# Graph layer, destination pass: record windows of 192 rows with two neighbouring rows on a partition

## What is computed

```python
# layer 0: attributes of the edges, summed at their source node
seg_sum, seg_max, cnt = segments of edge_attr (50000 x 32) by src
seg_mean = seg_sum / maximum(cnt, 1);  seg_max = where(cnt > 0, seg_max, 0)
x = x + relu(concat(seg_sum, seg_max, seg_mean, u) @ W1 + b1) @ W2 + b2
# layer 1: features of the source nodes, summed at the destination node
h = relu(layernorm(x))
x = x + relu(segment_sum(h[src], dst) @ W.T + b)
```

## Time and profile before

| | us |
|---|---|
| median of 3 runs | 1623.49 |
| lowest and highest run | 1609.49, 1625.28 |
| span of the profiled execution | 1619.7 |

### The profile page before, as it was taken

One profiled execution on the slowest core, in us unless ns is written; L12 is line 12 of the kernel. 1 busy time (PEld: TensorE's weight loads), 2 busy tenths in 40 slices (PEclk: granted clock), 3 DMA queues, 4 the chain that ended last, 5 costly groups with the idle time before them and its releaser, 6 DMA issues.

```text
span 1619.7 us, 28924 instructions
## 1 busy us (share of the span) xinstructions
PE 880.8 (54%) x8466; PEld 635.9 (39%) x8466; DVE 995.8 (61%) x2746; ACT 552.6 (34%) x1726; POOL 848.1 (52%) x863
## 2 busy tenths in 40 slices
PE   0120145787888788888795113545455445455553
PEld 0010022555555555565574102433334333333442
DVE  9899944677777777778795113444455444444553
ACT  0300123444444444444451213333344333333430
POOL 4733175566656666666610755555566555555400
PEclk9985556899989989889998555555555555555555
DMA  1000012688777877777797114787688767887889
GB/s 42 0 0 0 15 39 57 159 224 225 206 199 201 218 211 209 206 205 214 215 256 225 27 31 100 180 203 176 161 184 195 174 165 178 201 189 180 190 204 205
DMA packets 486483, 253.92 MB, mean 157 GB/s; under 512 B 417657, under 2 KB 449373, under 8 KB 486323
## 3 DMA queue, kind: packets, MB, share of 16 engines
q1 hardware_dynamic: 376066, 157.65, 39.3%
q10 hardware_dynamic: 85168, 75.08, 15.4%
q0 software_dynamic: 25088, 19.32, 7.0%
HBM read 159.45 MB, written 92.43 MB: 156 GB/s over the span
## 4 chain that ended last, share of the span: by engine, by line
ACT 20%; ACTq 19%; another core or an unknown queue 18%; issue 16%; DVE 15%; PE 9%; DMA 2%; SPq 1%; POOL 1%; DVEq 0%; POOLq 0%
ACTq L680 10%; ACT hn L759 6%; ACT xa L665 4%; ACTq L712 3%; ACTq L686 3%; ACT rec L706 3%; ACT hid L693 2%; ACTq L673 2%; DVE ka L976 2%; DVE kb L976 2%; ACT rec L700 2%; DVE ka L977 2%; DVE kb L977 1%; PE p_m L1428 1%
## 5 line engine op out<-in xcount | busy, mean ns | idle before, releaser
L589 POOL DMA_INDIRECT xa<-node_table,gi x392 | 370.7, 946 | 340.8 <-ACT hn L759 142.5
L577 POOL DMA_INDIRECT xa<-in_edge_attr_dram,gi x392 | 402.0, 1026 | 266.7 <-issue 94.9
L759 ACT ACTIVATE hn<-xa,nmr,rstd 128x64 f32<-128x64 f32 x392 | 140.4, 428 | 340.9 <-issue 292.0
L1228 DVE RECIPROCAL rstd<-sd 128x4 f32<-128x4 f32 x98 | 17.5, 178 | 303.9 <-ACT sd L751 210.5
L700 ACT CAST rec<-p_m 128x256 bf16<-128x256 f32 x164 | 60.7, 370 | 292.7 <-remote 259.6
L1480 PE MATMUL p_g<-ident,hn 128*128 128x128 f32 x196 | 64.9, 431 | 156.1 <-ACT hn L759 94.8
L1125 DVE TENSOR_TENSOR_SCAN feats<-c_rows,feats,p_g 64x512 f32<-64x512 f32 x97 | 122.9, 1267 | 16.4 <-PE p_g L1412 8.2
L693 ACT ACTIVATE hid<-p_z,bias_z 128x512 f32<-128x512 f32 x98 | 113.1, 1154 | 53.9 <-issue 23.2
L1428 PE MATMUL p_m<-w_s,hid 128*128 128x64 f32 x784 | 121.2, 300 | 6.6 <-issue 6.5
L1127 DVE TENSOR_TENSOR_SCAN feats<-c_rows,feats,p_g 32x512 f32<-32x512 f32 x97 | 123.3, 1271 | 1.4
L1420 PE MATMUL p_z<-feats,w_s 96*128 96x512 f32 x196 | 119.5, 695 | 3.4 <-DVE feats L1127 2.6
(11 more groups left out here) (277 smaller groups left out, 1820.1 us busy)
## 6 DMA issues: line engine op xcount, KB each, us to landing
records<-rec ACTq DMA_DIRECT2D x196, 196.0 KB
win<-records SPq DMA_DIRECT2D x392, 85.8 KB
node_table<-dout SPq DMA_DIRECT2D x49, 512.0 KB
din<-node_table SPq DMA_DIRECT2D x49, 512.0 KB
out_dram<-dout SPq DMA_DIRECT2D x49, 512.0 KB
din<-in_x_dram SPq DMA_DIRECT2D x48, 512.0 KB
c_rows<-rows_src ACTq DMA_DIRECT2D x141, 128.0 KB
win<-records SPq DMA_DIRECT2D x392, 42.9 KB
```

The source lines that it names most:

```text
L577: g.indirect_dma_start(out=xa[n % XRING][:, t, 0:FE], out_offset=None, in_=edge_attr, in_offset=bass.IndirectOffsetOnAxis(ap=gi[0][:, BT * ...
L589: g.indirect_dma_start(out=xa[k % XRING][:, t, :], out_offset=None, in_=T, in_offset=bass.IndirectOffsetOnAxis(ap=gi[1][:, BT * n + t:BT * ...
L759: last = s.activation(hn[n % 2][:, t, :], xa[k % XRING][:, t, :], ACT.Relu, bias=nmr[n % 2][:, t:t + 1], scale=rstd[n % 2][:, t:t + 1])
```

## The change

- A window now serves a pair of groups (256 nodes) and has 192 rows. Rows 2p and 2p + 1 of it stand on partition p, in two neighbouring slots of `win`, so 96 partitions (`PAIR`) are written. There are four such loads a block, all issued by SP. `upper_windows` is gone, and with it its place in ACT's loop, whose length falls by the four rounds that only served it.
- `start_row[1]` holds one start for each pair, packed together, and four of them are loaded into SP's registers a block.
- A row of either slot can belong to either group. So there are 16 one-hot matrices of 96 x 128 a block: eight slots, each compared with 0 to 255, in one DVE instruction of 96 x 2048.
- Each group sums over both slots of its pair and three parts: 8 x 2 x 3 = 48 products a block.
- The count before the pass looks for pairs with over 192 rows. The presets of the one-hots' partitions 96 to 127 follow the new shape, and `sign_out` shares its memory with `base_i`.

```diff
+PAIR = 96
-        base_i = sb("base_i", [P, GROUPS], I32)
+        scratch = sb("scratch", [P, GROUPS])
+        base_i, sign_out = scratch[:, :].bitcast(I32), scratch[:, 0:COLS]
-        oneh = [[sb(f"oneh{s}_{b_}", [P, *shape, UNIT], BF16) for b_ in range(HRING)] for s, shape in enumerate(((PER // 2, 3), (PER,)))]
+        oneh = [[sb(f"oneh{s}_{b_}", [P, *shape, UNIT], BF16) for b_ in range(HRING)] for s, shape in enumerate(((PER // 2, 3), (PER, 2)))]
         def win_count(k):
-            return sum(16 * PER // (2 if j < BLOCKS else 1) for j in range(k % WRING, k + 1, WRING))
+            return 16 * PER // 2 * (k // WRING + 1)
@@ windows(side, m)
-                starts = start_row[side][0:1, PER * m:PER * (m + 1) if side == 0 else PER * m + PER // 2]
+                starts = start_row[side][0:1, PER * m:PER * (m + 1)] if side == 0 else start_row[side][0:1, PER // 2 * m:PER // 2 * (m + 1)]
...
-                        sp.dma_start(win[g % WRING][0:WP, q, :], recs[side][bass.ds(at[q], WP), :]).then_inc(win_in[g % WRING], 16)
+                        sp.dma_start(win[g % WRING][0:PAIR, 2 * q:2 * q + 2, :],
+                                     recs[side][bass.ds(at[2 * q], 2 * PAIR), :].rearrange("(p a) r -> p a r", a=2)).then_inc(win_in[g % WRING], 16)
@@ block.gpsimd
-            link(g.tensor_copy(start_row[1][:, :], over[:, :]))
+            link(g.tensor_copy(start_row[1][:, 0:GROUPS // 2], over[:, 0:GROUPS:2]))
...
-            link(g.tensor_scalar(over[:, 0:LAST], over[:, 0:LAST], float(WP), None, ALU.is_gt))
+            link(g.tensor_scalar(over[:, 0:LAST // 2], over[:, 0:LAST // 2], float(2 * PAIR), None, ALU.is_gt))
...
             for t in oneh[1]:
-                link(g.tensor_copy(t[96:P, :, :], mask[1][96:P, 0:1].unsqueeze(2).to_broadcast([P - 96, PER, UNIT])))
+                link(g.memset(t[96:P, :, :, :], 0.0))
+                link(g.tensor_copy(t[96:P, 0:PER:2, :, :].rearrange("p s h n -> p s (h n)"),
+                                   mask[1][96:P, 0:1].unsqueeze(2).to_broadcast([P - 96, PER // 2, 2 * UNIT])))
@@ block.scalar, upper_windows(m)
-                for q in range(PER // 2):
-                    s.dma_start(win[g % WRING][0:WP, PER // 2 + q, :], recs[1][bass.ds(at[q], WP), :]).then_inc(win_in[g % WRING], 16)
...
-                for n in range(BLOCKS + DST_WIN):
+                for n in range(BLOCKS + DST_REC):
...
-                    if valid(n - DST_WIN):
-                        upper_windows(n - DST_WIN)
@@ relative(side, m), onehots(side, m)
-                    v.tensor_tensor(rel[k % 2][0:WP, :, :], win[k % WRING][0:WP, :, KEY].unsqueeze(2).to_broadcast([WP, PER, 2]),
...
+                v.tensor_tensor(rel[k % 2][0:rows, :, :].rearrange("p (q a) i -> p q a i", a=2),
...
-                    v.tensor_tensor(hot[0:WP, :, :].rearrange("p s (n i) -> p s n i", i=2),
-                                    nodes[:, 0:UNIT // 2, :].unsqueeze(1).to_broadcast([WP, PER, UNIT // 2, 2]),
-                                    rel[k % 2][0:WP, :, :].unsqueeze(2).to_broadcast([WP, PER, UNIT // 2, 2]), ALU.is_equal).then_inc(hot_ok, 1)
+                    v.tensor_tensor(hot[0:PAIR, :, :, :].rearrange("p s h (n i) -> p s (h n) i", i=2),
+                                    nodes[0:PAIR].unsqueeze(1).to_broadcast([PAIR, PER, UNIT, 2]),
+                                    rel[k % 2][0:PAIR, :, :].unsqueeze(2).to_broadcast([PAIR, PER, UNIT, 2]), ALU.is_equal).then_inc(hot_ok, 1)
@@ expand(side, m)
                     for s in range(PER):
-                        for w in range(3):
-                            last = mm(to[:, D * s:D * (s + 1)], oneh[1][m % HRING][:, s, :], win_words[k % WRING][:, s, D * w:D * (w + 1)],
-                                      start=w == 0, stop=w == 2)
+                        for a in range(2):
+                            slot = s // 2 * 2 + a
+                            for w in range(3):
+                                last = mm(to[:, D * s:D * (s + 1)], oneh[1][m % HRING][:, slot, s % 2, :], win_words[k % WRING][:, slot, D * w:D * (w + 1)],
+                                          start=a == 0 and w == 0, stop=a == 1 and w == 2)
```

More of the change, by code:

```diff
@@ L170, in build @@
         above = sb("above", [P, SPAN, GROUPS], F16)
-        sign_out = sb("sign_out", [P, COLS])
         over = sb("over", [1, GROUPS])
@@ L554, in _ @@
             link(g.tensor_tensor(over[:, :], limit[:, :], over[:, :], ALU.subtract))
-            link(g.tensor_copy(start_row[1][:, :], over[:, :]))
+            link(g.tensor_copy(start_row[1][:, 0:GROUPS // 2], over[:, 0:GROUPS:2]))
             link(g.tensor_scalar(over2[:, :], over2[:, :], 0.0, None, ALU.is_lt))
-            link(g.tensor_tensor(over[:, 0:LAST], start_f[:, 1:LAST + 1], start_f[:, 0:LAST], ALU.subtract))
-            link(g.tensor_scalar(over[:, 0:LAST], over[:, 0:LAST], float(WP), None, ALU.is_gt))
-            g.tensor_tensor(over[:, 0:LAST], over[:, 0:LAST], over2[:, 0:LAST], ALU.add).then_inc(s_rows1, 1)
+            link(g.tensor_tensor(over[:, 0:LAST // 2], start_f[:, 2:LAST + 1:2], start_f[:, 0:LAST:2], ALU.subtract))
+            link(g.tensor_scalar(over[:, 0:LAST // 2], over[:, 0:LAST // 2], float(2 * PAIR), None, ALU.is_gt))
+            g.tensor_tensor(over[:, 0:LAST // 2], over[:, 0:LAST // 2], over2[:, 0:LAST:2], ALU.add).then_inc(s_rows1, 1)
             pool.wait_ge(s_wts, 1)
@@ L667, in scale_attr @@
                 last.then_inc(scaled, 1)
-            def upper_windows(m):
-                g = BLOCKS + m
-                starts = start_row[1][0:1, PER * m + PER // 2:PER * (m + 1)]
-                _, at = nc.values_load_multi_w_load_instructions(starts, engines=[mybir.EngineType.Activation], min_val=0, max_val=E,
-                                                                 skip_runtime_bounds_check_because="each start is a count of rows, lowered to its limit on the chip")
-                for n in range(AHEAD + 1) if m == 0 else [min(m + AHEAD, BLOCKS - 1)]:
-                    stored = BLOCKS + n
-                    act.wait_ge(rec_out[stored % RRING], 16 * (stored // RRING + 1))
-                act.wait_ge(expanded, g - WRING + 1)
-                for q in range(PER // 2):
-                    s.dma_start(win[g % WRING][0:WP, PER // 2 + q, :], recs[1][bass.ds(at[q], WP), :]).then_inc(win_in[g % WRING], 16)
             def load_rows(k):
@@ L927, in beside_turn @@
                     dve.wait_ge(s_rows1, 1)
-                    v.reduce_sum(wrong[0:1, 1:2], over[:, 0:LAST], AX.X)
+                    v.reduce_sum(wrong[0:1, 1:2], over[:, 0:LAST // 2], AX.X)
                     v.tensor_scalar(wrong[0:1, 5:6], start_f[:, LAST:LAST + 1], float(E), None, ALU.not_equal)
@@ L1142, in relative @@
                 dve.wait_ge(win_in[k % WRING], win_count(k))
-                if side == 1:
-                    v.tensor_tensor(rel[k % 2][0:WP, :, :], win[k % WRING][0:WP, :, KEY].unsqueeze(2).to_broadcast([WP, PER, 2]),
-                                    base_f[0:WP, PER * m:PER * (m + 1)].unsqueeze(2).to_broadcast([WP, PER, 2]), ALU.subtract).then_inc(rel_ok, 1)
-                    return
-                v.tensor_tensor(rel[k % 2][0:WP, :, :].rearrange("p (q a) i -> p q a i", a=2),
-                                win[k % WRING][0:WP, :, KEY].rearrange("p (q a) -> p q a", a=2).unsqueeze(3).to_broadcast([WP, PER // 2, 2, 2]),
-                                base_f[0:WP, PER * m:PER * (m + 1):2].unsqueeze(2).unsqueeze(3).to_broadcast([WP, PER // 2, 2, 2]),
+                rows = WP if side == 0 else PAIR
+                v.tensor_tensor(rel[k % 2][0:rows, :, :].rearrange("p (q a) i -> p q a i", a=2),
+                                win[k % WRING][0:rows, :, KEY].rearrange("p (q a) -> p q a", a=2).unsqueeze(3).to_broadcast([rows, PER // 2, 2, 2]),
+                                base_f[0:rows, PER * m:PER * (m + 1):2].unsqueeze(2).unsqueeze(3).to_broadcast([rows, PER // 2, 2, 2]),
                                 ALU.subtract).then_inc(rel_ok, 1)
```

1 line of the change is left out of this document (added).

## The result

| | before | after |
|---|---|---|
| median, us | 1621.88 (1609.49 to 1625.28, 4 runs) | 1653.42 (1650.15 to 1656.36, 4 runs) |
| span of the profiled execution | 1619.7 | 1652.6 |
| ratio after to before | | 1.0233, 95% interval 1.0173 to 1.0294 |

The medians alone give 1.0194, which lies inside the interval.

The account below looks back on a forecast made before the run. ACT's queue with its window loads was taken to bound the destination pass; after, PE's 3.9 us plus 1.69 crawl plus 0.1 waiting give 5.7 us a block for 6.67, saving 83 us: 1540 us, range 1488 to 1625.

Parts of the forecast that it names:

- 1.69 us of crawl: Destination pass: PE's unexplained "issue" idle time before products and `conv`, 1.69 us a block, added unchanged to PE's new work.
- PE's busy time: Destination pass: 24 more products a block; 4.57 us at 1.2 GHz, 3.9 with a third of the time at 2.4 GHz.
- ACT: Destination pass: ACT loses `upper_windows`, 2.64 us of a 5.63 us iteration; its own floor becomes 3.0 us.
- DVE's one-hot: Destination pass: the 96x2048 one-hot takes about 1.22 us, 0.53 us more a block, at no cost while POOL covers it.
- POOL's floor: Destination pass: four gathers of 1.25 us make a hard floor of 5.0 us a block; at most 140 us gained.
- rival B: Clock doesn't rise and crawl stays as now: 6.5 us a block, 1609 us; chance 0.22.
- a faster PE falls back: TensorE's clock: longer bursts speak for a rise, but a faster PE idles half the step and drops back.
- SP: Destination pass: SP issues all windows, four loads a block; occupied up to 5.6 us a block, crawl included.
- DMA: Destination pass: all DMA falls from 5.14 to 4.4 us a block; 784 B window packets at 41 ns.
- D: Change doesn't do what it says: pieces stay at 392 B, or a pair exceeds 192 rows (under 1 in 100).
- C: Crawl goes by the PE instruction: 7.8 us a block, 1720 us, a loss from 2.1 us of crawl on; chance 0.15.
- A: POOL is the bound, as the clock rises or the crawl shrinks: 5.15 us a block, 1491 us; chance 0.20.

Follow-up runs that it names:

- x2: Kernel after without the second slot's products, 24 a block instead of 48; 1626.47 us, 0.9986 of before, on a chip with crawl.
- x4: Kernel before with each of its 24 products a block issued twice; 1683.92 us, 1.0312 of before, on a chip with crawl.
- y3: Kernel after with the source pass's 224-row windows, 12 one-hots and 36 products in the destination pass; 1641.18 us, 1.0119 of before, on a chip with crawl.
- z7: Kernel before with three of a block's four row gathers left out in the destination pass; 1481.20 us, 0.91 of before, on a chip with crawl.
- z4: Kernel after unchanged, on a chip without crawl; 1350.46 us, 0.9766 of before.
- x3: Kernel after with three of a block's four row gathers left out in the destination pass; 1396.85 us, 0.8564 of before, on a chip with crawl.
- z1: Kernel after with two of a block's four row gathers left out in the destination pass; 1275.96 us, 0.9218 of before, on a chip without crawl.
- z6: Kernel after with two of a block's four row gathers left out, again, on a chip with crawl; 1425.68 us, 0.8741 of before.

## Why the prediction was wrong, point by point

**The failed step: "1.69 us of crawl".** The prediction took the crawl as it stood in PE's idle time before products and `conv`, and added it to PE's new work as a constant. It measured 3.02 us with `turn_h`, 2.97 without. Two errors in one term. It wasn't the whole crawl even of before: with `turn_h` 2.18. And above all, as x2, x4 and y3 have it, it was what was left of the crawl after the part that fell into PE's waits for ACT and DVE, 1.15 us a block, had been hidden. The change took those waits away, and the crawl came out whole. x2 has it without the added products: 24 of them and four gathers as before, ACT relieved, and the step is 6.67 us as before. ACT's relief bought nothing there (SP's issuing all windows and the larger one-hots are in x2 too).

The difference of the steps: forecast 5.7, measured 7.25, 1.55 us. The crawl has 1.33 of them (3.02 against 1.69), PE's busy time 0.31 (4.21 against 3.9), less the 0.1 of waiting that didn't occur.

The other way round, from the undisturbed steps: before 5.63 (by the earlier trace rows; z7 has 5.68), after 5.29 (z4, on another chip). The change gains 0.34 us a block, which is also what the two times on chip D give, 35.2 us over 98 blocks. The crawl adds 1.04 to the first and 1.96 to the second, since in the second it lies on the path whole. 0.92 - 0.34 = 0.58 = 7.25 - 6.67.

**ACT: right.** L680 and L673 are gone, `hn` is no longer behind "issue" (37.6 us for 302.8). That it bought nothing is PE's doing, above. The Trainium skill (DMA: Bandwidth & Descriptors, Issuing engines are not separate DMA queues) says that issuing from several engines saves only sequencer time, "usually small". Here that time was 2.64 us of ACT in each iteration. x2's unchanged step agrees with the rule's outcome, and z4, where the change gains 2.3%, doesn't.

**DVE's one-hot: right**, 1218 ns for a forecast 1.22 us, and hidden. With a side effect that was not forecast: gathers that run beside a one-hot for over 0.5 us take 1.37 us in the mean, those beside none 0.96, and the mean of all rose from 946 to 1043 ns. POOL's floor of 5.0 us a block is 5.29 in z4. That counts where there is no crawl, 0.3 us of step.

**PE's busy time: nearly.** 4.21 us a block for 3.9; the granted clock 0.67 is just the third of the time at 2.4 GHz that was assumed, so that share was right and rival B's "no rise" is out. z4 shows that a PE with waits of some 3 us in the mean and 6.4 at most before its bursts still gets 0.80, so "a faster PE falls back" was too dark. The Trainium skill (TensorE: Matmul & The Clock Gate, Part 1) says that the clock falls after an idle time; no run here was made to test it.

**SP: right in size, wrong in use.** The prediction left out that SP also waited for `expanded` where a PE instruction is named as releaser, 38.1 us more in before, so it was occupied for up to 5.1 us a block and not 5.6. After, it waits 148 us for `expanded`, so it was not the bound. Its issues crawl beside PE's: eight take 10.7 to 11.4 us in 1100:1150, against 6.1 to 7.6 in z4.

**DMA: nearly.** 0.66 x 7.25 = 4.8 us a block, for 4.4; 4.87 in z4. The window packets have 784 bytes and are 96 for each of 308 loads, 383 a block, so the pair is one piece and D is out. They took 49 ns in the mean, where 41 was assumed. DMA bounds nothing until gathers are left out, at 4.9 us a step (x3, z1, z6).

**The rivals.** C's sign, crawl at 3 us before products, is there (2.88), and so is its outcome, a loss. Its deciding point of 2.1 us was worked out for a PE that is busy 4.57 us; with the 4.21 measured it is 2.46, and 3.02 is past either. Its mechanism was wrong, and so its size: by the instruction it would have been 3.12 too, but busy time of 4.57 at a clock that doesn't rise made it 7.8. The argument against C was that the source pass with more instructions crawls less. That argument was good against a price per instruction, and was then used as if it were one for a constant 1.69, which it isn't. A, which allowed for a crawl that shrinks, is what happens without crawl. What was missing as a case of its own: "the crawl is larger than what is seen of it", with a price from above. The rows had it: 6.28 us of ACT's wait in one iteration of the earlier trace rows, and a step of 6.67 beside an undisturbed 5.63.

**The start and the end.** The start holds its pace, 52 `hn` by 1000 us against 48. The end takes 4.9 us a block, as before (12 one-hots in 60 us, 5.0).

## What to carry to other kernels

Idle time that an engine shows under "issue" can be less than what slows it: a part that falls into its waits for others isn't seen, and can appear when those waits are taken away, as from 2.18 to 3.02 us here. So before a kernel's bound is moved onto an engine that starts its instructions late, take its disturbed stretches by themselves, ask what the time would be if the engine had work all the time, and price the change with that. Measure small gains on more than one chip where the profile holds a disturbance that nobody can name.

## What the runs showed of the hardware that was not expected

- The same kernel took 1628.5 to 1629.2 us on three chips and 1385.4 and 1385.7 on two, 15% less. The source pass too was slower on the former: 626 us in after's first trace from ACT's first `hid`, of which there is one a block, to its last (6.5 us a block), and 517 us in z4 (5.3), though PE's "issue" idle is only 28.3 us in 400 there.
- On the slower ones, with four indirect gathers a block, PE starts instructions 0.7 or 1.4 us apart for 3.0 to 3.3 us in each block (2.0 to 2.2 in the kernel before, where PE also waits for others), whether 24, 36 or 48 products are to be started, whether rows have 128 or 256 bytes, at a DMA share of 0.56 to 0.77. SP's issues are slowed beside it. With two gathers a block PE's crawl is 0.09 us. What else must be there is open: the source pass, with as many gathers per us, has little of it.
- A gather takes 944 ns where one a block is left (x3 946, z7 943), and 1.02 to 1.04 us in the mean beside a 96x2048 one-hot of 1.22 us on DVE.
